# A graph network in one launch on one core: the 13 of 55 groups of source scores that GpSimd gathers are made by products of one-hots as well

## The chip, the cores and the metric

The kernel runs on one core of a Trainium2 chip. The core has five engines with queues of their own: TensorE (PE; its weight loads are listed as PEld), VectorE (DVE), ScalarE (ACT), GpSimd (POOL) and SyncE (SP, which here only issues DMAs). DMAs issued by SP and by GpSimd share 16 DMA engines. The metric is the device time of one execution in microseconds (us), lower is better.

## The reference

A graph has 3125 nodes with 512 features and 53125 edges, sorted by target (`dst`). Four residual layers follow each other, each on `h = relu(layernorm(x))`:

```python
x = x + relu(segment_sum((h @ W0)[src] * edge_weight, dst))                  # layer 0
x = x + relu(segment_sum(norm * (h @ W1.T + b1)[src], dst))                  # layer 1
x = x + relu((h + segment_sum(h[src], dst)) @ G1 + g1) @ G2 + g2             # layer 2
# layer 3, for each of 8 heads:
Wx = h @ Ws[head] + Wb[head]
s = leaky_relu(Wx[dst] @ a_w[head, :64] + Wx[src] @ a_w[head, 64:] + a_b[head], 0.2)
alpha = exp(s - segment_max(s)[dst]); alpha = alpha / segment_sum(alpha)[dst]
out = segment_sum(alpha[:, None] * Wx[src], dst)
```

What matters here is `s` of layer 3: each edge needs 8 numbers of its target node and 8 numbers of its source node. They are called target scores and source scores below.

## The kernel before, in words

The nodes are split into 25 tiles of 125. The edges are split into 440 steps (`STEPS`) of 128 edges; a step belongs to one tile of targets. A layer runs over the 440 steps: GpSimd gathers the 128 source rows of a step from a table in memory with one indirect DMA into a ring of 11 buffers (L1758 in layers 0 to 2, L1813 in layer 3), VectorE builds the step's one-hot of targets, TensorE multiplies it into the tile's sum (L1456; L1452 and L1453 in layer 2). Layer 3 also multiplies the rows by the exponentials on VectorE (L1218).

Between the steps of layer 2 and those of layer 3 lies a stage that makes the scores of all edges; it is called the score stage here, and its loop the score loop. The 440 steps form 55 groups (`NG`) of 8 steps (`UG`).

- Target scores: SP loads a group's target places, repeated over 128 partitions (`load_dst`, L1915). ScalarE makes the one-hot of them in two operations (`dst_hot`, L1337 and L1341). TensorE multiplies it with the tile's scores (L1671), one matmul a step. VectorE sums the three bf16 parts of 20 steps at once (`target_sum`, L1078). There are 22 such sums.
- Source scores, by products: a node number is split into a place (0 to 111) and a column (0 to 27, itself two digits). SP loads a group's digits, repeated over 123 partitions (`load_src`, L1923, three DMAs). VectorE makes the one-hot (`src_hot`, L1052). TensorE multiplies it with a table of 28 x 8 columns in which all columns but the right one get a very negative number (`source_product`, L1687): for a pair of steps 2 x 3 matmuls of 224 columns. VectorE takes the maximum over the 28 columns (`source_max`, L1093), once for a pair of steps, four times for a group. The banks of a pair are used again four pairs later.
- Source scores, by gathering: GpSimd gathers 8 numbers a row with one indirect DMA a step from the table of scores in memory (L1791), straight into `ue`, where the maxima go too.

Before the change the groups with `k % 4 == 3` (`GATHERED`, 13 of them, 104 steps) are gathered, the other 42 (`PRODUCTS`) are products. GpSimd issues the 104 gathers one after another when the node rows of layer 3 are done (it waits for `pj_out` and `u_st`). TensorE's, VectorE's and ScalarE's loops of this stage are written out by hand: `for k in range(NP)` runs over the product groups, and the 440 target steps are spread evenly over their pairs (`targets_till`), so that 55 target groups go with 42 source groups. The target loop of ScalarE runs over all 55 groups.

The scores of a block of 110 steps (`RS`; four blocks) are turned by TensorE with 32 matmuls (L1703, L1704) and worked on by VectorE in two halves of five operations (`edge_scores`, L1102 to L1115). `SCORES_FROM` says at which product group that begins for the first three blocks; the fourth follows the loop. TensorE waits for a block's maxima (`u_sum`), target sums (`te_sum`) and gathers (`got_u`) before it turns it.

After its score gathers GpSimd fetches 25 steps' rows of layer 3 ahead, into the space of `x` (L1805). It waits for the last load of source digits before the first of them, and for all one-hots (`dp_ok`, `sp_ok`) before the last four. The gathers of the ring (L1813) wait for the end of the fourth block (`end_rows`, VectorE L1144).

Of the kernel before, what the change touches and what calls it, by code (L numbers as in the profile page):

```python
# [26 lines left out]
def build(nc, x_in, src_in, dst_in, w_in, W0_in, W1_in, b1_in, G1_in, g1_in, G2_in, g2_in,  # L27
# [5 lines left out]
    TILES = N // TN  # L33
# [3 lines left out]
    RB = 4  # L37
    RS = STEPS // RB
# [13 lines left out]
    UG = 8  # L52
    NG = STEPS // UG
# [5 lines left out]
    PAIRS = UG // 2  # L59
# [1 line left out]
    TCS = STEPS // TC  # L61
    TH = TILES * H

    PRODUCTS = [k for k in range(NG) if k % 4 != 3]
    GATHERED = [k for k in range(NG) if k % 4 == 3]
    NP = len(PRODUCTS)
    NB = 4
    SCORES_FROM = (13, 23, 34)
    SLOPE = 0.2
    XQ = TILES // 5  # L70
    LOADED = 8
# [32 lines left out]
    with ctx:  # L104
# [3 lines left out]
        def signal(name):  # L108
            return ctx.enter_context(nc.semaphore(name))

        V, A, P, G, S = nc.vector, nc.scalar, nc.tensor, nc.gpsimd, nc.sync
# [6 lines left out]
        src_digits = nc.dram_tensor("src_digits", (3, STEPS, CE), BF16, kind="Internal").ap()  # L118
        kept_x = nc.dram_tensor("kept_x", (TILES, TN, D), F32, kind="Internal").ap()
        score_table = nc.dram_tensor("score_table", (N, H), F32, kind="Internal").ap()  # L120
# [15 lines left out]
        src_t = sb("src_t", [CE, STEPS], I32)  # L136
# [63 lines left out]
        def z16(n):  # L200
# [12 lines left out]
                          for n in range(2))  # L213
# [43 lines left out]
        ue = big[:, 4 * FW:4 * FW + STEPS * H].rearrange("p (i h) -> p i h", h=H)  # L257
# [6 lines left out]
        dp, sp, dp_hot, sp_hot = ([flat_acc[:, 2 * WR + (2 * n + q) * GW // 2:2 * WR + (2 * n + q + 1) * GW // 2].bitcast(BF16)  # L264
                                   for q in range(2)] for n in range(4))
# [66 lines left out]
        g2_tr, g2_rows, g2_z = (signal(f"g2_{n}") for n in ("tr", "rows", "z"))  # L332
# [5 lines left out]
        pj_tr, pj_hi, pj_lo, pj_z, pj_out = (signal(f"pj_{n}") for n in ("tr", "hi", "lo", "z", "out"))  # L338
# [24 lines left out]
        u_st = [signal(f"u_st{n}") for n in range(2)]  # L363
# [4 lines left out]
        far_ok = signal("far_ok")  # L368
        dp_ok, sp_ok = signal("dp_ok"), signal("sp_ok")
        te_mm, te_sum = signal("te_mm"), signal("te_sum")  # L370
        got_u = [signal(f"got_u{n}") for n in range(RB)]
        u_mm, u_sum = signal("u_mm"), signal("u_sum")
        cont_ok, cont_rep = signal("cont_ok"), signal("cont_rep")
        sc_mm, sc_z = signal("sc_mm"), signal("sc_z")
# [43 lines left out]

        def pair_step(n):

            return PRODUCTS[n // PAIRS] * UG + 2 * (n % PAIRS)

        def pairs_till(i):
            return sum(pair_step(n) < i for n in range(NP * PAIRS))

        def targets_till(n):

            return STEPS * n // (NP * PAIRS)

# [7 lines left out]
        def vector_program():  # L437
# [681 lines left out]
            beside = {}  # L1119
            for b, f in enumerate(SCORES_FROM):  # L1120
                for half in range(2):
                    scores = edge_scores(b, half)
                    for k in range(f + 3 + 2 * half, f + 5 + 2 * half):
                        beside[k] = [scores]
            for k in range(NP + 1):
                if k + 1 < NP:
                    src_hot(k + 1)
                for pair in range(PAIRS):
                    n = k * PAIRS + pair
                    if k:  # L1130
                        source_max(n - PAIRS)
                    if k < NP:
                        target_steps(targets_till(n), targets_till(n + 1))
# [268 lines left out]
        def tensor_program():  # L1402
# [115 lines left out]
            for i in range(STEPS + 14):  # L1518
# [9 lines left out]
                k = ended.get(i - 10)  # L1528
# [6 lines left out]
                k = ended.get(i - 13)  # L1535
# [94 lines left out]
            for i in range(STEPS):  # L1630
                step(2, i)
                for lag, work in ((6, turn_sums), (13, first_product), (27, turn_first), (34, second_product), (48, turn_last),
                                    (55, score_product), (Z_AT, rows_product)):
                    k = ended.get(i - lag)
# [56 lines left out]
            def edge_scores(b, half, part):  # L1691

                if half == part == 0:
                    P.wait_ge(pj_out, 3 * TILES)
                    P.wait_ge(te_sum, te_chunks(b))
                    P.wait_ge(u_sum, pairs_till((b + 1) * RS))
                    P.wait_ge(got_u[b], 16 * sum(i // RS == b for k in GATHERED for i in range(k * UG, (k + 1) * UG)))
                h0 = half * 4
                if b and part == 0:
                    P.wait_ge(sc_z, 2 * b + half - 1)  # L1700
                for j in (2 * part, 2 * part + 1):
                    to = bank[6 + half][0:RS, j * CE:(j + 1) * CE]
                    P.matmul(to, ue[:, b * RS:(b + 1) * RS, h0 + j], ident[:, :], start=True, stop=False)  # L1703
                    last = P.matmul(to, te[:, b * RS:(b + 1) * RS, h0 + j], ident[:, :], start=False, stop=True)  # L1704
                if part:
                    last.then_inc(sc_mm, 1)
# [43 lines left out]
        def gpsimd_program():  # L1750
            own = Order(g_own)

            def gather(layer):
                for i in range(STEPS):
                    n = STEPS * layer + i
                    if n >= RING:
                        G.wait_ge(stepped, step_value(n - RING))
                    G.indirect_dma_start(  # L1758
                        out=(ring16 if layer == 2 else ring)[:, n % RING, :], out_offset=None, in_=table[layer][:, :],
                        in_offset=bass.IndirectOffsetOnAxis(ap=src_t[:, i:i + 1], axis=0)).then_inc(got[n % RING], 16)  # L1760

            G.memset(ident[:, :], 0.0).then_inc(setup, 1)
            G.wait_ge(setup, 1)
            G.affine_select(out=ident[:, :], in_=ident[:, :], compare_op=ALU.not_equal, fill=1.0, base=0,
                            pattern=[[-1, 128]], channel_multiplier=1).then_inc(setup, 1)
            G.iota(iota_i[:, :], pattern=[[1, TN]], base=0, channel_multiplier=0).then_inc(setup, 1)
            G.iota(step_i[:, :], pattern=[[RS, RB]], base=0, channel_multiplier=1).then_inc(setup, 1)
            G.iota(place_i[:, :], pattern=[[0, 1]], base=0, channel_multiplier=1).then_inc(setup, 1)
            G.iota(tile_i[:, :], pattern=[[CE, TILES - 1]], base=CE, channel_multiplier=0).then_inc(setup, 1)
            G.wait_ge(step_no, 2)  # L1770
            G.wait_ge(rows_out, 16)
            for b in range(RB):
                G.indirect_dma_start(
                    out=step_rows[b].bitcast(I32), out_offset=None, in_=edge_rows[:, :],
                    in_offset=bass.IndirectOffsetOnAxis(ap=gstep[:, b:b + 1], axis=0)).then_inc(rows_in, 16)

            G.wait_ge(tables, 6)
            G.wait_ge(rows_turned, 1)
            for layer in range(3):
                for n in range(TILES * layer + TILES - 3, TILES * (layer + 1)):  # L1780
                    G.wait_ge(table_st[n % 3], table_value(n))
                gather(layer)


            for q in range(2):
                G.wait_ge(u_st[q], 16 * len(range(q, TILES, 2)))
            G.wait_ge(g2_z, TILES)
            G.wait_ge(pj_out, 3 * TILES)
            for k in GATHERED:
                for i in range(k * UG, (k + 1) * UG):  # L1790
                    G.indirect_dma_start(  # L1791
                        out=ue[:, i, :], out_offset=None, in_=score_table[:, :],
                        in_offset=bass.IndirectOffsetOnAxis(ap=src_t[:, i:i + 1], axis=0)).then_inc(got_u[i // RS], 16)


            G.wait_ge(x_kept, 32 * TILES)
            for q in range(NB):
                G.wait_ge(sp_in[q], 48 * len(range(q, NP, NB)))
            for n in range(4 * TILES - 3, 4 * TILES):
                G.wait_ge(table_st[n % 3], table_value(n))  # L1800
            for k, i in enumerate(AHEAD):
                if k == TILES - 4:
                    G.wait_ge(dp_ok, NG)
                    G.wait_ge(sp_ok, NP)
                G.indirect_dma_start(  # L1805
                    out=rows_at(i), out_offset=None, in_=table[3][:, :],
                    in_offset=bass.IndirectOffsetOnAxis(ap=src_t[:, i:i + 1], axis=0)).then_inc(got_x[AHEAD.index(i) // XQ], 16)
            G.wait_ge(end_rows, 2)
            for k, i in enumerate(ring_steps):
                n = ring_use(i)  # L1810
                if k >= RING:
                    G.wait_ge(stepped, step_value(3 * STEPS + ring_steps[k - RING]))
                G.indirect_dma_start(  # L1813
                    out=rows_at(i), out_offset=None, in_=table[3][:, :],
                    in_offset=bass.IndirectOffsetOnAxis(ap=src_t[:, i:i + 1], axis=0)).then_inc(got[n % RING], 16)

        def sync_program():
# [24 lines left out]
            for a, arr in enumerate((src_in, dst_in, w_in)):  # L1842
                e = edf if a == 2 else ed
# [72 lines left out]
                            .to_broadcast([128, GW])).then_inc(dp_in[k % NB], 16)  # L1916

            def load_src(k):
                g = PRODUCTS[k]
                if k >= NB:  # L1920
                    S.wait_ge(sp_ok, k - NB + 1)
                for a, (p0, p1) in enumerate(((0, SPL), (SPL, SA), (SA, SK))):
                    S.dma_start(sp[k % NB][p0:p1], src_digits[a, g * UG:(g + 1) * UG, :].rearrange("(a i) e -> a (i e)", a=1)  # L1923
                                .to_broadcast([p1 - p0, GW])).then_inc(sp_in[k % NB], 16)


# [94 lines left out]
```

## Time and profile before

| | us |
|---|---|
| median of 3 timed runs | 2626.45 (2623.59 to 2630.86) |
| span of the profiled execution | 3086.3 |
| of it: up to the first gather of layer 0 | 118 |
| layers 0 to 2, first to last gather | 1954 |
| score stage, last gather of layer 2 to first ring gather of layer 3 | 381 |
| layer 3 | 634 |

The profiled execution took 17.5% longer than the timed ones; no time of that execution other than its span is given. TensorE is busy in 77% of the span, GpSimd in 58%, VectorE in 52%, ScalarE in 11%. These are averages over stages that are limited in different ways: read each stage by itself, by cutting it into stretches. The busy time of GpSimd is that of issuing its DMAs. Idle time is put down either to the instruction that ended it or to "issue", when the engine waited for nothing that the profile shows.

### The profile page before, as it was taken

What the parts mean: (1) busy time and instruction counts of PE and PEld (TensorE: products, weight loads), DVE (VectorE), ACT (ScalarE), POOL (GpSimd) and SP (SyncE); (2) the same over time, 40 slices, a digit from 0 to 9 for tenths busy, and PEclk for the clock granted to TensorE, in tenths of its full rate; (3) what the DMA queues carried; (4) which work ended last, traced back from release to release, by engine and by line L of the source; (5) the groups of instructions that cost most, each with busy time, mean ns of one, the idle gap of its engine ahead of it and who ended that gap; (6) DMA issues with size and microseconds to landing.
All of it is one profiled execution on the core that took longest, in us unless ns stands there. A gap on an engine that the chain in (4) does not pass through costs nothing.

```text
span 3086.3 us, 32808 instructions
## 1 busy us (share of the span) xinstructions
PE 2384.8 (77%) x8542; PEld 1265.4 (41%) x8542; DVE 1593.7 (52%) x3774; ACT 335.0 (11%) x523; POOL 1795.9 (58%) x1878
## 2 busy tenths in 40 slices
PE   7888889887678777785788888885068589988887
PEld 5534444343223222221354454453058445544444
DVE  7665555554234353332244444444059677766665
ACT  4200000000000000000000000001057310000000
POOL 0466666665466666665666666653710456666665
PEclk9898999998789888997899999997579789999999
DMA  6586666676567766666666666663134457776665
GB/s 157 174 243 180 174 180 177 187 241 177 154 192 212 203 201 205 196 193 181 184 200 198 204 200 199 204 181 80 10 101 153 136 157 211 208 222 192 194 190 171
DMA packets 212761, 557.12 MB, mean 181 GB/s; under 512 B 55433, under 2 KB 56834, under 8 KB 212601
## 3 DMA queue, kind: packets, MB, share of 16 engines
q0 software_dynamic: 144448, 462.60, 52.3%
q1 hardware_dynamic: 66970, 90.10, 9.7%
q10 hardware_dynamic: 1182, 2.33, 0.3%
q8 instruction: 96, 1.57, 0.2%
q14 instruction: 65, 0.52, 0.1%
HBM read 515.28 MB, written 39.59 MB: 180 GB/s over the span
## 4 chain that ended last, share of the span: by engine, by line
PE 51%; DVE 15%; another core or an unknown queue 13%; issue 12%; DMA 6%; POOL 2%; ACT 1%; SPq 0%; ACTq 0%; DVEq 0%; POOLq 0%
PE tiles L1456 28%; DMA ring<-table,src_t 5%; PE upper L1416 5%; PE last_bank L1597 2%; PE tiles L1453 2%; PE tiles L1452 2%; DVE sel L776 2%; PE upper L1458 2%; PE last_bank L1416 2%; PE upper L1687 1%; POOL ring L1758 1%; PE upper L1626 1%; PE upper L1405 1%; DVE stage L713 1%
## 5 line engine op out<-in xcount | busy, mean ns | idle before, releaser
L1758 POOL DMA_INDIRECT ring<-table,src_t x1320 | 1266.9, 960 | 717.8 <-issue 324.3
L1456 PE MATMUL tiles<-ring,sel 128*125 128x512 f32 x2590 | 1390.4, 652 | 264.2 <-issue 178.4
L1456 PEld LDWEIGHTS tiles<-ring,sel 128*125 128x125 f32 x2590 | 444.3, 198 | 754.6 <-issue 745.5
L1813 POOL DMA_INDIRECT ring<-table,src_t x415 | 399.0, 961 | 240.5 <-PE upper L1458 105.5
L483 DVE TENSOR_TENSOR sel<-iota_bank,dl_t 128x500 f32<-128x500 f32 (+1 forms) x330 | 221.5, 674 | 513.3 <-PE tiles L1456 226.6
L1218 DVE TENSOR_TENSOR ring<-ring,last_bank 128x512 f32<-128x512 f32 x388 | 260.5, 685 | 169.6 <-DMA ring<-table,src_t 140.6
L1458 PEld LDWEIGHTS upper<-big,sel 128*125 128x125 f32 x880 | 169.7, 193 | 222.5 <-issue 222.0
L1452 PE MATMUL tiles<-ring,sel 128*125 128x512 f16 x440 | 176.5, 401 | 61.8 <-issue 32.1
L1453 PE MATMUL tiles<-ring,sel 128*125 128x512 f16 x440 | 172.9, 393 | 10.6 <-issue 10.3
L1416 PE MATMUL upper<-wh,hTh 128*125 128x512 f32 x200 | 100.4, 502 | 73.1 <-DVE hTl L759 23.7
L1791 POOL DMA_INDIRECT big<-score_table,src_t x104 | 98.4, 946 | 81.5 <-DVE acc L988 50.1
L776 DVE TENSOR_SCALAR sel<-node_iota,dl_t,w_t 128x125 f32<-128x125 f32 x440 | 134.2, 358 | 0.3 <-PE tiles L1456 0.2
L1458 PE MATMUL upper<-big,sel 128*125 128x8 f32 x880 | 126.2, 215 | 0.6 <-issue 0.6
L713 DVE TENSOR_TENSOR stage<-iota_bank,stage 128x500 bf16<-128x500 f32 x110 | 74.3, 676 | 86.5 <-remote 60.4
L1805 POOL DMA_INDIRECT x<-table,src_t x25 | 26.3, 1052 | 155.5 <-DMA acc<-src_digits 144.6
L1452 PEld LDWEIGHTS tiles<-ring,sel 128*125 128x125 f16 x440 | 61.2, 139 | 130.0 <-issue 111.8
L1597 PE MATMUL last_bank<-big,stage 128*125 128x512 f32 x200 | 96.8, 629 | 8.9 <-issue 7.3
L1093 DVE TENSOR_REDUCE big<-upper 128x16 f32<-128x448 f32 x84 | 50.6, 618 | 83.7 <-remote 72.4
L1405 PE MATMUL upper<-ident,stage 125*128 125x125 f32 x400 | 61.6, 277 | 41.2 <-ACT stage L1231 20.6
L1416 PE MATMUL upper<-wl,hTh 128*125 128x512 f32 x200 | 93.3, 466 | 0.0
L1416 PE MATMUL upper<-wh,hTl 128*125 128x512 f32 x200 | 92.1, 461 | 0.0
L1416 PEld LDWEIGHTS upper<-wh,hTh 128*125 128x125 f32 x200 | 45.9, 230 | 98.2 <-issue 85.0
(335 smaller groups left out, 2522.2 us busy)
## 6 DMA issues: line engine op xcount, KB each, us to landing
ring<-table,src_t POOLq DMA_INDIRECT x1735
table<-stage SPq DMA_DIRECT2D x50, 224.0 KB
table<-acc SPq DMA_DIRECT2D x50, 224.0 KB
acc<-dst_places SPq DMA_DIRECT2D x28, 256.0 KB
x<-dst_places SPq DMA_DIRECT2D x27, 256.0 KB
x<-in_x SPq DMA_DIRECT2D x25, 224.0 KB
kept_x<-x SPq DMA_DIRECT2D x25, 224.0 KB
x<-kept_x SPq DMA_DIRECT2D x25, 224.0 KB
```

Source lines behind the costliest of these rows:

```text
L483: V.tensor_tensor(to, iota_p[:, None, :].to_broadcast([CE, SB, TN]), dl_t[:, i:i + SB, None].to_broadcast([CE, SB, TN]), ALU.is_equal).the ...
L713: V.tensor_tensor(lo_hot[:, i % (2 * SB):i % (2 * SB) + SB, 0:TN], iota_p[:, None, :].to_broadcast([CE, SB, TN]), s_lo[:, i:i + SB, None]. ...
L776: V.tensor_scalar(out=sel[:, i % SELS, :], in0=node_iota[:, :], scalar1=dl_t[:, i:i + 1], scalar2=w_t[:, i:i + 1], op0=ALU.is_equal, op1=A ...
L1218: V.tensor_tensor(slot, slot, weights[:, :, None].to_broadcast([CE, H, DP]), ALU.mult).then_inc(scaled, 1)
L1416: last = P.matmul(to, a[:, q, k, :], b[:, k, :], start=(k == 0 and n == 0), stop=(k == KB - 1 and n == 2))
L1452: P.matmul(to, sel16[:, n % SELS, :], ring16[:, r, 0:D], start=False, stop=True, skip_group_check=True)
L1453: last = P.matmul(to, sel16[:, n % SELS, :], ring16[:, r, D:2 * D], start=False, stop=True, skip_group_check=True)
L1456: last = P.matmul(to, sel[:, n % SELS, :], rows, start=False, stop=True, skip_group_check=True)
L1458: last = P.matmul(upper[0:TN, bass.ds(b, 1), DEN_AT:DEN_AT + H].rearrange("p a h -> p (a h)"), sel[:, n % SELS, :], exps[:, i, :], start=F ...
L1597: last = P.matmul(bank[7][0:TN, :], yT[:, b, :], raw_w[:, b, :], start=(b == 0), stop=(b == KB - 1))
L1758: G.indirect_dma_start(out=(ring16 if layer == 2 else ring)[:, n % RING, :], out_offset=None, in_=table[layer][:, :], in_offset=bass.Indir ...
L1813: G.indirect_dma_start(out=rows_at(i), out_offset=None, in_=table[3][:, :], in_offset=bass.IndirectOffsetOnAxis(ap=src_t[:, i:i + 1], axis ...
```

## The change

All 55 groups are made by products. `NP`, the number of product groups, goes from 42 to 55; the list of gathered groups, GpSimd's 104 gathers with their waits, and TensorE's waits for them are taken out. The blocks of scores begin at groups 16, 30 and 44 of 55, where they began at 13, 23 and 34 of 42. The loops that run over `NP` now run over 55 groups, and the target steps are spread over 220 pairs, where they were spread over 168.

```diff
-    PRODUCTS = [k for k in range(NG) if k % 4 != 3]
-    GATHERED = [k for k in range(NG) if k % 4 == 3]
-    NP = len(PRODUCTS)
+    NP = NG
     NB = 4
-    SCORES_FROM = (13, 23, 34)
+    SCORES_FROM = (16, 30, 44)
...
-        got_u = [signal(f"got_u{n}") for n in range(RB)]
...
         def pair_step(n):
-            return PRODUCTS[n // PAIRS] * UG + 2 * (n % PAIRS)
+            return 2 * n
...
                     P.wait_ge(te_sum, te_chunks(b))
                     P.wait_ge(u_sum, pairs_till((b + 1) * RS))
-                    P.wait_ge(got_u[b], 16 * sum(i // RS == b for k in GATHERED for i in range(k * UG, (k + 1) * UG)))
...
-            for q in range(2):
-                G.wait_ge(u_st[q], 16 * len(range(q, TILES, 2)))
-            G.wait_ge(g2_z, TILES)
-            G.wait_ge(pj_out, 3 * TILES)
-            for k in GATHERED:
-                for i in range(k * UG, (k + 1) * UG):
-                    G.indirect_dma_start(
-                        out=ue[:, i, :], out_offset=None, in_=score_table[:, :],
-                        in_offset=bass.IndirectOffsetOnAxis(ap=src_t[:, i:i + 1], axis=0)).then_inc(got_u[i // RS], 16)
...
             def load_src(k):
-                g = PRODUCTS[k]
                 if k >= NB:
                     S.wait_ge(sp_ok, k - NB + 1)
                 for a, (p0, p1) in enumerate(((0, SPL), (SPL, SA), (SA, SK))):
-                    S.dma_start(sp[k % NB][p0:p1], src_digits[a, g * UG:(g + 1) * UG, :]...
+                    S.dma_start(sp[k % NB][p0:p1], src_digits[a, k * UG:(k + 1) * UG, :]...
```

## Rows read from the trace of the kernel before

**Rows 1.** The page: the slices of the whole span, 77 us each
```profile
PE   7888889887678777785788888885068589988887
POOL 0466666665466666665666666653710456666665
PEclk9898999998789888997899999997579789999999
```
**Rows 2.** Busy time by stretch: us, PE, PEld, DVE, ACT, POOL, clock, DMA share, GB/s
```profile
2072.00:2453.00 381.00, 210.80 (x1728) 171.30 (x1729) 188.14 (x369) 130.11 (x127) 125.91 (x131) 0.75 0.34 93
2138.00:2268.00 130.00, 13.21 (x49) 5.09 (x49) 4.14 (x7) 5.41 (x6) 86.86 (x92) 0.50 0.10 11
2268.00:2397.00 129.00, 116.47 (x1225) 109.11 (x1226) 115.54 (x208) 99.48 (x96) 0.00 (x0) 0.92 0.50 154
```
**Rows 3.** Timeline of the score stage, PE and POOL, inside the first of these stretches
```profile
2219.04 0.35 PE L1687 MATMUL tiles<-stage,acc 123*128 123x224 bf16 x1 [1.76 <-issue]
2219.26 0.94 POOL L1791 DMA_INDIRECT big<-score_table,src_t  x1 [0.30 <-issue]
2220.51 0.94 POOL L1791 DMA_INDIRECT big<-score_table,src_t  x1 [0.30 <-issue]
2221.14 0.10 PEld L1687 LDWEIGHTS tiles<-stage,acc 123*128 123x128 bf16 x1 [3.39 <-issue]
2222.54 0.34 PE L1687 MATMUL tiles<-stage,acc 123*128 123x224 bf16 x1 [3.15 <-issue]
```
**Rows 4.** Instructions by line: all gathers, duration min/median/max in ns, first and last start
```profile
L1758 POOL DMA_INDIRECT ring<-table,src_t x1320: 940/946/1642, 117.8 to 2071.9; - x189
L1791 POOL DMA_INDIRECT big<-score_table,src_t x104: 940/944/1133, 2122.9 to 2251.7; - x104
L1813 POOL DMA_INDIRECT ring<-table,src_t x415: 940/946/3199, 2452.6 to 3073.0; - x139
```
**Rows 5.** Waits of GpSimd: us in total, times, longest
```profile
POOL ring L1758 <- DMA table<-stage: 45.5, 2, 29.7
POOL ring L1758 <- DMA table<-acc: 29.7, 1, 29.7
```
**Rows 6.** Timeline of one product group on VectorE, first to next one-hot, and PE's pairs
```profile
2377.57 0.48 DVE L1052 TENSOR_SCALAR acc<-acc,digit 123x1024 bf16<-123x1024 bf16 x1
2377.97 0.62 DVE L1093 TENSOR_REDUCE big<-tiles 128x16 f32<-128x448 f32 x1
...
2378.19 0.73 PE L1687 MATMUL upper<-stage,acc 123*128 123x224 bf16 x6
...
2378.50 0.61 DVE L1093 TENSOR_REDUCE big<-iota_bank 128x16 f32<-128x448 f32 x1
...
2378.81 0.73 PE L1687 MATMUL upper<-stage,acc 123*128 123x224 bf16 x6
...
2379.56 0.65 DVE L1078 TENSOR_REDUCE ring<-tiles 128x160 f32<-128x480 f32 x1
...
2380.13 0.61 DVE L1093 TENSOR_REDUCE big<-upper 128x16 f32<-128x448 f32 x1
...
2380.66 0.48 DVE L1052 TENSOR_SCALAR acc<-x,digit 123x1024 bf16<-123x1024 bf16 x1
```
**Rows 7.** Busy time by stretch: 30 product groups, and six without scores between
```profile
2277.28:2389.41 112.13, 101.53 (x1088) 95.48 (x1087) 103.24 (x186) 88.93 (x84) 0.00 (x0) 0.94 0.52 159
2282.91:2300.71 17.80, 16.63 (x210) 15.93 (x208) 17.09 (x35) 17.54 (x17) 0.00 (x0) 1.00 0.66 206
```
**Rows 8.** Timeline: one half block of scores on VectorE, first and last of five operations
```profile
2447.45 0.68 DVE L1102 SCALAR_TENSOR_TENSOR acc<-acc 110x512 f32<-110x512 f32 x1
...
2451.27 0.69 DVE L1115 TENSOR_TENSOR acc<-acc,ring 110x512 f32<-110x512 f32 x1
```
**Rows 9.** DMA queues: 2150 to 2240 us, and 2282 to 2302 us
```profile
q0 software_dynamic: 2303, 0.30, 8.6%
...
q1 hardware_dynamic: 2274, 4.00, 63.6%
```
**Rows 10.** Timeline of VectorE: the fourth one-hot of the loop
```profile
2133.34 0.48 DVE L1052 TENSOR_SCALAR acc<-x,digit 123x1024 bf16<-123x1024 bf16 x1
```
**Rows 11.** The chain of waits, pairs of source products after a wait for VectorE
```profile
2328.16 1.21 PE iota_bank L1687 x6
2329.45 1.13 PE upper L1687 x6
2330.62 1.13 PE upper L1687 x6
```
**Rows 12.** Timeline: GpSimd's first gather ahead, its 22nd, and a one-hot beside them
```profile
2397.29 1.42 POOL L1805 DMA_INDIRECT x<-table,src_t  x1 [144.64 <-DMA acc<-src_digits]
...
2401.13 0.46 DVE L1052 TENSOR_SCALAR acc<-x,digit 123x1024 bf16<-123x1024 bf16 x1
...
2424.96 0.94 POOL L1805 DMA_INDIRECT x<-table,src_t  x1 [0.30 <-issue]
```

More of the change, by code:

```diff
@@ L1922, in load_src @@
                 for a, (p0, p1) in enumerate(((0, SPL), (SPL, SA), (SA, SK))):
-                    S.dma_start(sp[k % NB][p0:p1], src_digits[a, g * UG:(g + 1) * UG, :].rearrange("(a i) e -> a (i e)", a=1)
+                    S.dma_start(sp[k % NB][p0:p1], src_digits[a, k * UG:(k + 1) * UG, :].rearrange("(a i) e -> a (i e)", a=1)
                                 .to_broadcast([p1 - p0, GW])).then_inc(sp_in[k % NB], 16)
```

## The prediction

> **What bounds the kernel now.** I read the slices of the whole span first [rows 1]. TensorE is busy nearly everywhere except in three slices near two thirds, where it falls to 5, 0 and 6 tenths while GpSimd stands at 3, 7 and 1. That is the score stage, the only place that the change touches. Then I cut this stage into stretches [rows 2]. From the last gather of layer 2 to the first ring gather of layer 3 it takes 381 us. In it lie two opposite halves: 130 us in which TensorE starts only 49 matmuls and its clock is at 0.50 (1.2 GHz), and 129 us in which it starts 1225. The reader is to see that the first of them is exactly the time of the 104 score gathers (2122.9 to 2251.7, [rows 4]), with some 15 us of delay at either end.
>
> The timeline shows what TensorE does there [rows 3]: single weight loads and matmuls, 1.4 to 3.4 us apart, each put down to "issue", so they wait for no semaphore. VectorE and ScalarE only wait for TensorE. GpSimd issues a gather every 1.25 us (0.94 and a gap of 0.30) without a hitch. So in the profiled execution the gathers stop TensorE. Forty-nine matmuls are 49/1088 of 112.13 us [rows 7], 5 us of work, so this costs 125 us.
>
> **Is that time there in a timed run?** The whole forecast hangs on this, because the profiled execution has a span of 3086.3 us and the timed runs a median of 2626.45. The sum can be drawn up from GpSimd, which paces the layers. Its steady pitch is 1.25 us (more exactly 0.944 + 0.303 = 1.247). Layers 0 to 2 have 1320 gathers, 1646 us, and waits for tables between layers of 29.7 us, twice or so: 60 us [rows 4, 5]. Layer 3 has 415: 518 us. With 118 us before the first gather and 13 us after the last (3086.3 less 3073.0), everything but the score stage takes 2355 us at least. The timed median leaves 272 us for the score stage, where the profile shows 381. The difference is 109 us, close to the 125 of the stretch in which TensorE is stopped. If the stage took 381 us in a timed run, the total would be 2736 us. The other reading needs the gathers to be faster without a profile: at 1.185 us a gather the sum closes with a score stage of 381. No row gives such a pitch, while 1.247 is the pitch of the whole first stretch. I take the stopped time for a property of the profiled execution at 87 in 100.
>
> The Trainium skill, page "NOTIFIC — the notification-queue block", section 7.1, says that the block which writes the trace's records holds its producers back inside rather than lose a record. If that is what stops TensorE, the stop is in no timed run, which is the reading taken; no run here shows it yet.
>
> **The score loop without the stop.** Its pace is read where no gather runs. From one one-hot at 2277.28 to the 31st at 2389.41 there are 30 groups in 112.13 us, 3.74 us each [rows 7]. In it are blocks of scores: one half block takes 2447.45 to 2451.99 (the last starts at 2451.27 and lasts 0.69), 4.5 us [rows 8], so three whole blocks in the loop are 27 us. Where no scores lie between, six groups take 17.80 us, 2.97 us each. One group on VectorE [rows 6]: one-hot 0.40 (2377.57 to 2377.97) and four maxima of 0.53 (2377.97 to 2378.50), 2.53 us, and half a target sum: 0.57 (2379.56 to 2380.13) x 22/42 = 0.30. That is 2.83 of the 2.97. VectorE is busy in 17.09 of those 17.80 us, but ScalarE in 17.54: it makes 55/42 target one-hots a source group. So the pitch has 0.14 us that VectorE waits, and two engines are about even there. TensorE needs 0.63 to 0.65 a pair (2378.19 to 2378.81), 2.6 a group, and is third.
>
> **The change part by part.**
> - *Added, 13 groups on VectorE*: 13 x 2.53 = 32.9 us, all in the loop's pace. The target sums and score blocks stay as they are in number.
> - *Given back*: ScalarE now has one target group a source group, at most 17.54/17.80 x 2.97 x 42/55 = 2.2 us against 2.53 + 0.57 x 22/55 = 2.76 us on VectorE. The 0.14 us a group should go: 42 x 0.14 = 5.9 us. Sum: +27 us.
> - *Added on TensorE*: 13 x 24 matmuls, 13 x 2.6 = 34 us, beside VectorE's. TensorE then needs 4 x 0.65 = 2.6 us a group, under 2.76. This cover is thin: if it goes, the loop is TensorE's (second rival).
> - *Added on SP*: 13 x 3 loads of digits, by the same depth of four buffers. The DMA queue of SP has 63.6% of the engines where the loop runs freely [rows 9]; a source group brings 55/42 fewer target loads with it afterwards, so the rate falls. Nothing.
> - *Removed, 104 gathers of 32 bytes a row*: 130 us of GpSimd. Without the stop, is anything waiting for them? The fourth one-hot of the loop starts at 2133.34 [rows 10], the gathers at 2122.9. At 1.25 us they end at 2253, and land a few us later. The 42 groups end at 2133.34 + 38 x 2.97 + 27 = 2273. The earlier blocks ask for 24, 52 and 80 gathers, done at 2153, 2188 and 2223; the loop gets to groups 13, 23 and 34 at about 2163, 2202 and 2243. Every one is 10 to 20 us early. They take 8.6% of the DMA engines [rows 9]. Between nothing and 8.6% of the loop's 42 x 2.97 = 125 us, 0 to 10.7 us, can come back; I take 2, the end with free DMA engines being nearer.
> - *TensorE's wait for the gathers, `got_u`*: met early, as above; nothing. The moved starts of blocks keep their place relative to the steps; nothing.
> - *Gathers ahead (L1805)*: they wait for the last load of digits before and after, so they move with the end of the loop. 22 of them take 2397.29 to 2425.90, 1.30 us each [rows 12], and layer 3's ring begins 27 us later. Nothing.
>
> Sum for a timed run: 32.9 - 5.9 - 2 = +25, so 2626.45 + 25 = 2651 us. Its ends: nothing given back and the pitch of 3.74 us a group of the whole stretch, 13 x 3.74 = 48.6, so 2675; and 32.9 - 5.9 - 10.7 = 16.3, so 2643. Against the profiled execution's own time the same sum is 3086.3 - 125 + 27 = 2988 us.
>
> **The rivals.**
> - *The stop is real* (the other side). The gathers stop TensorE in timed runs too. Then the change takes away 125 us and adds 27: 2626 - 98 = 2528 us. It decides as soon as more than 27 us of the 125 are in the timed runs. For it: it stands in the trace, and TensorE alone is hit, also beside the gathers ahead. Against it: the sum above. Chance 0.13.
> - *TensorE at its lower clock becomes the bound.* After VectorE's score work TensorE comes back at pairs of 1.17 us (2329.45 to 2330.62) [rows 11], against 0.65. If such spells grow, the added groups cost 13 x 4 x 1.17 = 61 us: 2687 us. Against it: the clock is 1.00 in the free stretch. Chance 0.05.
> - *The gathers were late in timed runs.* Beside a busy VectorE 22 of them took 1.30 us each, with single ones at 1.42 [rows 12]. At 1.30 they end at 2258, still ahead of 2273; the loop is theirs from (2273 - 2123)/104 = 1.44 us on. At 1.62 us they end at 2292, 19 us late, the change costs only 25 - 19 = 6 us: 2632, no change that can be told. Chance 0.12.
>
> To this last one the page "SBUF — State Buffer" of the Trainium skill speaks, in "SBUF: two separate sides": VectorE in its two-port modes and GpSimd lock each other out of a shared pair of ports. By that rule one-hots and gathers would slow each other, which speaks for this rival. The trace hardly agrees: a one-hot beside gathers took 0.46 us, one without 0.48 [rows 6, 12].
>
> **How the numbers follow.** A measurement of this kernel can tell about 0.3%, 8 us. The forecast, 2651, has 0.70, the clock 0.05, late gathers 0.12, the real stop 0.13. Slower by over 0.3%: 0.75; within: 0.12; faster: 0.13. The range takes the forecast's own, 2643 to 2675, and goes down over the late gathers to 2618; it leaves out the stop (0.13) and the clock (0.05).
>
> **What the profile afterwards would show.** The stop from 2138 to 2268 is gone, TensorE starts some 9 matmuls a us through the loop, and the profiled span falls by about 98 us although the timed runs get longer; that pair of signs is the test of the main step. The one-hots follow each other at about 2.76 us where no scores lie between, and ScalarE has idle time there. The gathers ahead still slow TensorE at the end of the loop. The prediction is wrong if the timed runs fall with the span, or if the pitch stays at 2.97 or rises because TensorE has taken the lead.

## The result, and the profile after

The changed kernel takes 2659.06 us (2653.42 to 2662.41, 4 runs) beside 2628.05 us of the kernel before: a ratio of 1.0119, with a 95% interval of 1.0101 to 1.0137. It is slower by 31 us, where 25 us were forecast. That is the answer on the chip of this comparison. On another chip, met later, the same change makes the kernel 3% faster, and that is the larger part of what follows: the stop of TensorE in the first profile [rows 2, 3] is real on chips of that kind, and absent on this one.

The page of the changed kernel, slices of 66.5 us:

```profile
PE   6889999989688888888589999999889699998898
DVE  7686666665335454333245555555799878877776
POOL 0277777777477777777577777775000567777775
PEclk9889999999899999999789999999999799999999
```

The hole of TensorE near two thirds [rows 1] is not there, and its clock stays up. GpSimd has nothing to do in the score stage. The span is 2661.1 us, that of the times. It fell by 425 us against the first profile, though the times rose; the prediction named that pair of signs, but expected a fall of only 98 us. The experiments give the reason: there are two kinds of chip, and the first profile looks like one of the slower kind, while the times were taken on the faster. The chip of the first profile is not on record. So the pair of signs tests nothing, and the kernel before needs a second profile (the first experiment) for a comparison. Busy time by stretch of that profile (first) and of the changed kernel (second), columns as in [rows 2]: the whole score stage, from the last gather of layer 2 to the first ring gather of layer 3, and 130 us inside its loop.

```profile
1844.70:2079.00 234.30, 192.03 (x1724) 165.09 (x1723) 185.82 (x364) 130.13 (x127) 134.66 (x131) 0.93 0.55 151
1908.00:2038.00 130.00, 115.99 (x1261) 109.87 (x1260) 116.53 (x210) 102.89 (x100) 95.30 (x93) 0.96 0.62 165
```

```profile
1839.30:2103.50 264.20, 221.95 (x2037) 194.44 (x2036) 218.75 (x429) 130.13 (x127) 26.44 (x26) 0.95 0.50 145
1910.00:2040.00 130.00, 117.42 (x1266) 111.10 (x1264) 122.22 (x224) 86.76 (x84) 0.00 (x0) 0.97 0.51 150
```

The stage grows from 234.3 to 264.2 us, by 29.9, nearly all of the 31. Inside the loop TensorE starts 1261 matmuls in 130 us with 93 gathers beside it, and 1266 without them; in the first profile it started 49 in such a stretch. The other parts stay: layers 0 to 2 take 1726.9 us (117.8 to 1844.7) before and 1722.2 us (117.1 to 1839.3) after. The spans differ by less than the medians (2637.2 and 2661.1 us), because the profiled execution of the kernel before took 2638.5 us, 10 more than its median, and 5 of them lie in those layers.

A piece of the loop on VectorE, in the timeline of the changed kernel:

```profile
1907.69 0.48 DVE L1049 TENSOR_SCALAR acc<-x,digit 123x1024 bf16<-123x1024 bf16 x1
1908.08 0.62 DVE L1090 TENSOR_REDUCE big<-tiles 128x16 f32<-128x448 f32 x1
1908.61 0.65 DVE L1075 TENSOR_REDUCE ring<-tiles 128x160 f32<-128x480 f32 x1
...
1910.77 0.48 DVE L1049 TENSOR_SCALAR acc<-x,digit 123x1024 bf16<-123x1024 bf16 x1
1910.94 0.31 PE L1668 MATMUL tiles<-stage,acc 125*128 x2 [0.71 <-issue]
1911.16 0.62 DVE L1090 TENSOR_REDUCE big<-tiles 128x16 f32<-128x448 f32 x1
1911.98 0.62 DVE L1090 TENSOR_REDUCE big<-iota_bank 128x16 f32<-128x448 f32 x1 [0.19 <-PE iota_bank L1684]
...
1913.77 0.48 DVE L1049 TENSOR_SCALAR stage<-acc,digit 123x1024 bf16<-123x1024 bf16 x1
```

The first group has a target sum (L1075) and takes 3.08 us. The next has none and still takes 3.00: TensorE stood for 0.71 us at a target matmul, and VectorE had to wait for its maximum. From 1907.69 to 1945.74 there are 13 groups of 2.93 us each, where 2.76 were expected. Six of the 13 have a target sum, where 5.2 are the average; that is 0.04 us a group of the difference.

### The profile page after: what moved, and what is told of

Read it like the earlier page. It is cut to its first block, busy times and chain, and to the rows that moved or that the text cites. A ratio compares the mean times of both kernels' runs of the same rounds, so it can differ in the third digit from the quotient of the medians.

```text
span 2661.1 us, 33494 instructions
## 1 busy us (share of the span) xinstructions
PE 2304.7 (87%) x8854; PEld 1231.9 (46%) x8854; DVE 1630.1 (61%) x3839; ACT 335.2 (13%) x523; POOL 1708.5 (64%) x1774
## 4 chain that ended last, share of the span: by engine, by line
PE 54%; DMA 19%; POOL 10%; DVE 9%; issue 7%; ACT 1%; SPq 0%; ACTq 0%; DVEq 0%; POOLq 0%
PE tiles L1453 30%; DMA ring<-table,src_t 18%; POOL ring L1754 9%; PE upper L1413 5%; PE last_bank L1413 3%; PE tiles L1449 3%; PE last_bank L1594 3%; PE tiles L1450 2%; PE upper L1684 2%; POOL ring L1798 2%; PE upper L1455 1%; PE upper L1402 1%; DVE big L1090 1%; PE iota_bank L1684 1%; PE upper L1623 1%
## 5 line engine op out<-in xcount | busy, mean ns | idle before, releaser
L1453 PE MATMUL tiles<-ring,sel 128*125 128x512 f32 x2590 | 1361.6, 635 | 174.4 <-DMA ring<-table,src_t 108.7
L1453 PEld LDWEIGHTS tiles<-ring,sel 128*125 128x125 f32 x2590 | 417.6, 190 | 667.1 <-issue 659.0
L1413 PE MATMUL upper<-wh,hTh 128*125 128x512 f32 x200 | 91.2, 456 | 3.4 <-DVE hTl L467 1.8
L1594 PE MATMUL last_bank<-big,stage 128*125 128x512 f32 x200 | 90.0, 592 | 1.6 <-DVE x L715 1.6
L1265 ACT ACTIVATE acc<-tiles,dis 125x512 f32<-125x512 f32 x25 | 17.2, 687 | 552.6 <-PE tiles L1453 552.6
L1267 ACT ACTIVATE acc<-tiles 125x512 f32<-125x512 f32 x25 | 14.9, 598 | 541.5 <-PE tiles L1450 541.5
L1263 ACT ACTIVATE acc<-tiles 125x512 f32<-125x512 f32 x25 | 14.9, 598 | 536.4 <-PE tiles L1453 536.4
L1413 PE MATMUL upper<-wl,hTh 128*125 128x512 f32 x200 | 81.4, 407 | 0.0
L1413 PE MATMUL upper<-wh,hTl 128*125 128x512 f32 x200 | 81.2, 406 | 0.0
```

The costliest lines, as they stand in the source:

```text
L1413: last = P.matmul(to, a[:, q, k, :], b[:, k, :], start=(k == 0 and n == 0), stop=(k == KB - 1 and n == 2))
L1453: last = P.matmul(to, sel[:, n % SELS, :], rows, start=False, stop=True, skip_group_check=True)
L1594: last = P.matmul(bank[7][0:TN, :], yT[:, b, :], raw_w[:, b, :], start=(b == 0), stop=(b == KB - 1))
```

## The experiments

The line numbers of a variant differ by a few from those of the kernel it starts from. The runs fell on four chips, each met once. On one of them the kernel before takes 2631 us (2624 to 2635 in 23 runs); on three it takes 3118, 3089 and 3120 us (3084 to 3128 in 38 runs). The first is called the faster kind below, the others the slower kind; whether that is a property of the chip or of a state that it was in, the runs can't tell. A ratio is always to the kernel before on the same chip.

**A second profile of the kernel before.** Nothing is edited.

> The kernel before, unchanged, to have a second profile of it beside its times. My theory (the stop of TensorE beside the score gathers belongs to the one profiled execution of 3086 us, not to the kernel): a span near 2627 us, TensorE runs through the 104 gathers at some 9 matmuls a us, one-hots 2.97 us apart where no scores lie between, the score loop ends at least 10 us after the last gather has landed. Rival (the stop is real, as the chance of 0.13 had it): the 130 us with some 49 matmuls are there again, whatever the span.

2628.86 us, 0.9994 (0.9985 to 1.0004). Instructions by line, and the waits of TensorE from 1900 to 2065 us:

```profile
L1791 POOL DMA_INDIRECT big<-score_table,src_t x104: 939/947/2349, 1893.9 to 2030.4; - x104
L1093 DVE TENSOR_REDUCE big<-upper x84: 592/612/626, 1902.8 to 2064.3; 128x16 f32<-128x448 f32 x84
L1805 POOL DMA_INDIRECT x<-table,src_t x25: 945/949/1782, 2039.2 to 2073.2; - x25
```

```profile
PE tiles L1671 <- issue: 11.8, 17, 2.0
PE tiles L1687 <- DVE big L1093: 10.3, 4, 6.6
PE upper L1687 <- DVE big L1093: 1.3, 2, 0.7
```

There is no stop and no wait for a gather. The last gather starts at 2030.4, the last maximum at 2064.3: the gathers are 34 us early by their starts, some 30 if one takes 3.8 us to land as a gather of the ring does, and not 20. Two sizes were off and nearly cancelled: a gather costs 1.33 us beside a busy VectorE (136.5 us for 103 intervals), not 1.25, and the loop from the fourth one-hot (1903.8) to the end takes 161 us, not 140.

**The gathers alone, in both kernels.** First, the kernel before without them:

```diff
                 for i in range(k * UG, (k + 1) * UG, 4):
-                    G.indirect_dma_start(out=ue[:, i, :], ...)
+                    G.memset(ue[:, i:i + 4, :], 0.0).then_inc(got_u[i // RS], 1)
```

> The kernel before with its 104 score gathers replaced by 26 fills with zeros on GpSimd: 42 groups of products, 13 groups of source scores that are not computed. It prices the gathers alone. My theory (hidden work that takes a small share of the DMA engines): 2628 - 2 us, anything from 2617 to 2629. Rival (the gathers were late for the scores, or held TensorE or VectorE up): the loop gets shorter by more than 11 us, 2617 us or less.

2630.7 us, 1.0001 (0.9992 to 1.0010): the gathers cost nothing that the times can tell; the interval still holds the 2 us that the sum gave back for them. The profiled score stage is 233.1 us (1836.2 to 2069.3) beside 234.3. Then the changed kernel with them:

```diff
+            for n, i in enumerate(i for k in range(3, NG, 4) for i in range(k * UG, (k + 1) * UG)):
+                if n >= 8:
+                    G.wait_ge(got_junk[n % 8], 16 * (n // 8))
+                G.indirect_dma_start(out=junk[:, n % 8, :], ...)
```

> The changed kernel, all 55 groups by products, with the 104 gathers put back: same place on GpSimd, same table and rows, but into a small tile that nobody reads, each waiting for the one eight before. It adds the gathers where nobody waits for them. My theory: 2659 + 2 us, at most 2670. Rival (beside a loop that VectorE and TensorE fill, gathers cost by ports or DMA engines, so that the change gave back more than 2 us): 2670 us or more.

2662.37 us, 1.0117 (1.0102 to 1.0131) beside 1.0119 of the changed kernel: again nothing that can be told. Its score stage is 266.4 us (1839.9 to 2106.3) beside 264.2. On this chip the change is 13 groups of products in exchange for something that costs some 1 to 2 us by the traces.

**More gathers: 18 groups.**

```diff
-    PRODUCTS = [k for k in range(NG) if k % 4 != 3]
+    PRODUCTS = [k for k in range(NG) if k % 3 != 2]
-    SCORES_FROM = (13, 23, 34)
+    SCORES_FROM = (12, 21, 30)
```

> The other way round: 18 of 55 groups gathered (every third) and 37 by products; the scores of the blocks begin at groups 12, 21 and 30. 40 gathers more than before, 50 us at 1.25 us each, and 5 product groups fewer. My theory (the gathers were about 20 us early before, so they become the bound): the last block waits for them, 50 - 20 = 30 us later, 2658 us. Rival (gathers are hidden at this number too, only products cost): 5 x 2.97 = 15 us less, 2613 us.

2647.3 us, 1.0068 (1.0055 to 1.0081): 18 us slower, not 30. The waits of TensorE, 1880 to 2110 us, and GpSimd's waits in the ring of layer 3, in the second profile of the kernel before and in this run:

```profile
PE upper L1703 <- DMA big<-score_table,src_t: 33.9, 3, 22.1
```

```profile
POOL ring L1813 <- PE upper L1458: 63.5, 149, 18.3
```

```profile
POOL ring L1813 <- PE upper L1458: 46.0, 148, 1.0
```

Here the gathers are the bound: TensorE stands 22.1 us at the last block of scores until they have landed. GpSimd goes on to its gathers ahead and to the ring without a pause between, and layer 3 begins 39 us later than before (a stage of 273.4 us, 1835.1 to 2108.5). But 21 of them come back in layer 3, 536.9 us instead of 558.2: the one wait of 18.3 us that GpSimd had there, once the ring was full, is gone. The sum of 30 us left this slack out: 40 gathers at 1.31 us are 52 us, and in the kernel before GpSimd waits 7.8 us before its gathers ahead, 4.9 after them and 18.3 in the ring. That leaves 21, near the 18 measured.

**Who paces the loop of 55 groups.** The maxima of the changed kernel over half the columns, and two of the three parts of each product. Both fell on a chip of the slower kind (3118 us), so the first was run again beside the changed kernel on another of that kind (3089 us):

```diff
-  bank[2 + n % 4][:, 0:2 * CTH].rearrange("p (i t h) -> p i h t", i=2, h=H),
+  bank[2 + n % 4][:, 0:2 * CTH].rearrange("p (i t h) -> p i h t", i=2, h=H)[:, :, :, 0:CT // 2],
```

```diff
-                    for part in range(3):
+                    for part in range(2):
```

> The changed kernel with the maxima of the source scores (L1090) taken over 14 of the 28 columns: the same 220 operations of VectorE over half the numbers, so part of the maximum is left out. It asks who paces the loop with 55 groups. Price on VectorE: 224 of 448 numbers, some 0.23 us of each 0.53, 220 times, 51 us. My theory (VectorE paces, TensorE is right behind with 2.52 us a group and its stalls at the loading of tile numbers, about 2.75 in all against 2.93 measured): only 10 to 20 us come back, 2640 to 2650 us. Rival (VectorE alone paces): some 50 us, 2610 us.

> The changed kernel with two of the three bf16 parts of each source product (L1684): 16 instead of 24 matmuls a group, the lowest part of the scores is left out. A pair then takes TensorE about 0.44 instead of 0.63 us. My theory (VectorE paces): only the stalls go, at most 55 x 0.2 = 10 us, 2649 to 2657 us. Rival (TensorE has taken the lead, the thin cover of the prediction): 220 x 0.19 = 42 us, 2617 us.

> The changed kernel with maxima over 14 of 28 columns, as in e4_half_max (part of the maximum is left out), now beside the changed kernel itself on the same chip. My theory as there (VectorE paces, TensorE is right behind): 10 to 20 us under the changed kernel. Rival (VectorE alone paces): 50 us under it.

Half the maxima: 0.9636 (0.9606 to 0.9666) and, again, 0.9637 (0.9611 to 0.9664), beside 0.9692 (0.9669 to 0.9716) of the changed kernel on that chip; 2978.04 beside 2994.57 us, 16.5 us less. Two parts: 0.9677 (0.9643 to 0.9711), which would be 5 us less; the intervals, taken on different chips, don't tell that from nothing nor from 20 us. The traces are closer: the score stage is 284.5 us in the changed kernel, 272.3 and 270.8 with half the maxima, and 287.9 with two parts. So taking away a third of TensorE's source matmuls gives nothing, far from the 42 us of the rival, and taking away 51 us of VectorE (0.39 instead of 0.62 us, 220 times) gives 16.5. VectorE paces and TensorE is right behind, as expected. Stretches inside the loop, of two parts and of half the maxima (again):

```profile
2172.00:2302.00 130.00, 101.86 (x1008) 91.97 (x1005) 125.06 (x233) 90.43 (x87) 0.00 (x0) 0.91 0.52 157
```

```profile
2170.00:2290.00 120.00, 114.13 (x1219) 109.83 (x1215) 91.74 (x216) 80.04 (x76) 1.78 (x2) 1.00 0.50 151
```

In the first VectorE is busy in 125.1 of 130 us, in the second TensorE in 114.1 of 120: each is full when the other is relieved.

**Less work for ScalarE**, on the kernel before:

```diff
-                own.mark(A.activation(dp[k % NB][0:TN], dp[k % NB][0:TN], ACT.Abs, bias=less_place[0:TN, :]))
-                A.wait_ge(a_own, own.n)
```

> The kernel before without the first of the two ScalarE operations of a target one-hot (L1337): ScalarE has about 1.1 us less for each of 55 groups, and the target one-hots come out wrong. It tests the term of the prediction that ScalarE held the loop of 42 groups up by 0.14 us a group. As predicted: 42 x 0.14 = 6 us less, 2623 us. Rival (ScalarE was only nearly as busy and held nobody up, and the 5.9 us were never there to be given back): 2629 us, no change.

3113.84 us beside 3118.35, 0.9986 (0.9969 to 1.0002). It fell on a chip of the slower kind, and its interval holds both the 6 us and none. Its trace settles the term all the same: 130 us from 15 us after the first score gather on, then the same 30 groups and the same six as in [rows 7].

```profile
2162.00:2292.00 130.00, 13.38 (x50) 5.17 (x50) 4.14 (x7) 3.31 (x4) 86.98 (x92) 0.51 0.08 10
2301.80:2413.99 112.19, 101.62 (x1088) 95.53 (x1087) 103.24 (x187) 46.85 (x44) 0.00 (x0) 0.94 0.51 159
2307.43:2325.23 17.80, 16.64 (x210) 15.94 (x208) 17.09 (x35) 9.23 (x9) 0.00 (x0) 1.00 0.69 212
```

The six groups take 17.80 us with ScalarE busy for 9.23 of them, and took 17.80 with ScalarE busy for 17.54; the 30 groups take 112.19 and took 112.13. ScalarE held nobody up. The first line shows another thing: this kernel is the kernel before but for one operation of ScalarE, it takes 3108 to 3123 us in its 12 runs, and its TensorE starts 50 matmuls in 130 us beside the gathers, as the first profile has 49. Its score stage takes 384.7 us (2093.0 to 2477.7), there it was 381. That is why the first profile is taken for one of a chip of the slower kind.

**15 groups gathered.**

```diff
-    PRODUCTS = [k for k in range(NG) if k % 4 != 3]
+    PRODUCTS = [k for k in range(NG) if k % 11 not in (3, 6, 10)]
-    SCORES_FROM = (13, 23, 34)
+    SCORES_FROM = (13, 23, 33)
```

> 15 of 55 groups gathered (three of each eleven), 40 by products; scores of the blocks begin at groups 13, 23 and 33. Two product groups fewer than before, 16 gathers more. In the second profile of the kernel before, GpSimd has some 33 us to spare on its way to the first rows of layer 3 that are used: 9 us before its gathers ahead, 6 after them, 18 when the ring is full; 16 gathers at 1.32 us take 21 of it. My theory (GpSimd's slack covers them, products cost 2.5 us a group): 5 us less than before, 2624 us. Rival (the last block of scores or the gathers ahead come late at once): 2630 us or more.

3133.61 us, 1.0045 (1.0025 to 1.0064), on the same chip as the last. What it would do on the faster kind stays open. On this one it is 14 us slower, and a sum fits that: 16 gathers more prolong the stop by 16 x 1.25 = 20 us, two product groups fewer give back 5.

**The changed kernel beside the kernel before on a chip of the slower kind.** Nothing is edited.

> The changed kernel, unchanged, beside the kernel before on whatever chip comes. The last four kernels met a chip on which the kernel before takes 3118 us in all its runs and TensorE is stopped beside the 104 score gathers, as in the first profile. My theory (the stop belongs to some chips, there it is in every run): on such a chip the change takes off about 125 us and adds 30, some 3025 us, 0.97 of the kernel before; on a chip of the other kind 2659 us, 1.012. Rival (the change costs 30 us everywhere, and the stop is made up elsewhere): 1.01 on either kind.

2994.57 us beside 3088.57: 0.9692 (0.9669 to 0.9716), 94 us faster. The score stage and 130 us inside its loop:

```profile
2068.30:2352.80 284.50, 226.56 (x2037) 196.65 (x2036) 219.78 (x431) 130.14 (x127) 26.00 (x26) 0.91 0.46 135
2150.00:2280.00 130.00, 118.45 (x1272) 112.54 (x1269) 122.13 (x224) 83.98 (x79) 0.00 (x0) 0.97 0.51 151
```

The stage takes 284.5 us, against 381 in the first profile [rows 2], which has the span and the stop of this kind of chip: 96 us less. Without gathers the loop runs on this chip as it does on the other, 1272 matmuls in 130 us beside 1266. The 20 us that the stage is longer than there come at its end, where the 25 gathers ahead run: the last one-hot follows the one before it after 21.6 us (2306.0 to 2327.7), on the faster kind after 3.2.

**The gathers put back on such a chip, and the gathers spaced.** First the changed kernel with 104 gathers that nobody waits for, the same edit as above; then the kernel before with a pause after each gather:

```diff
                         in_offset=bass.IndirectOffsetOnAxis(ap=src_t[:, i:i + 1], axis=0)).then_inc(got_u[i // RS], 16)
+                    G.memset(pause[:, :], 0.0).then_inc(paused, 1)
+                    pauses += 1
+                    G.wait_ge(paused, pauses)
```

> The changed kernel with the 104 score gathers put back into a tile that nobody reads, as in e2_55_and_gathers, in the hope of a chip of the slower kind (kernel before near 3090 to 3120 us). Nothing waits for these gathers there, so what they cost is neither a wait nor lateness. My theory (the gathers themselves stop TensorE on such a chip): about 115 to 125 us over the changed kernel's 0.969 of the kernel before, so 1.006 to 1.010 of it, some 3110 to 3120 us. Rival (it is the wait for the gathers that holds TensorE): 0.97. On a chip of the faster kind 1.012 again.

> The kernel before with a fill of a small tile (128 x 128) after each of the 104 score gathers, which GpSimd waits for: gathers some 1.7 instead of 1.25 us apart, so that they end some 45 us later. On a chip of the slower kind: if TensorE is stopped because gathers follow each other without a gap, it runs part of the time now and the kernel gains up to 50 us on the kernel before, 0.985 or less. Rival (each gather costs TensorE its time, whatever lies between): the stop is as large or lasts longer, 1.00 or more. On a chip of the faster kind the gathers eat up the slack and the kernel is 5 to 15 us longer than before.

3141.17 us, 1.0077 (1.0048 to 1.0105), and 3089.15 us, 0.9906 (0.9875 to 0.9937), beside 3119.82 us. The stretch of the gathers in the one and in the other:

```profile
2140.00:2270.00 130.00, 16.18 (x112) 11.38 (x112) 10.06 (x20) 9.27 (x10) 96.28 (x102) 0.54 0.19 35
```

```profile
2155.00:2295.00 140.00, 66.81 (x434) 46.56 (x433) 37.65 (x66) 39.74 (x41) 112.80 (x192) 0.56 0.25 61
```

In the first nothing waits for the gathers, and TensorE is stopped all the same: 112 matmuls in 130 us, 69 of them in the first 16 us, before it sets in. The gathers raise the ratio from 0.9692 to 1.0077, some 120 us. It is the gathers that stop TensorE, not a wait. In the second the gathers are 1.46 us apart (2143.2 to 2293.8 for 103 intervals) instead of 1.25 (1.7 were expected), and TensorE starts 3.1 matmuls a us instead of 0.4, unevenly: up to 75 in 8 us, and then again 16 to 20. It is still far from the 9.8 of a loop without gathers. The kernel gains 31 us by having GpSimd do more. The other reading, that each gather costs TensorE its time whatever lies between, falls; but three quarters of the stop are still there, and no run says how large a gap ends it.

## Why the prediction was right, and where not

*Sign and size on the chip of the comparison* were right: 31 us against 25, inside 2643 to 2675 and not far off its middle.

*Thirteen groups at 2.53 us* was the step that carried it, and it held: from the fourth one-hot to the last there are 38 groups in 148.8 us before (1903.8 to 2052.6) and 51 in 181.1 us after (1898.4 to 2079.5), 32.3 us for 13 groups, 2.48 each. (Against the kernel without gathers, 147.6 us, it is 33.5 and 2.58.) After the last one-hot the loop needs 2 us less than before, which makes 29.9.

*Given back by ScalarE, 5.9 us*, was the term that was mis-sized: it is nothing. ScalarE was busy in 17.54 of 17.80 us there [rows 7], and that was taken for holding VectorE up. With half of ScalarE's work taken away the same groups take the same 17.80 us, and in the changed kernel it is busy in 86.8 of 130 us and the groups still take 2.93. VectorE's one wait in those 17.80 us is 0.50 us for a product of TensorE, and TensorE's pauses before target matmuls are there in both kernels (6.7 us in those 30 groups before, 8.3 us in 51 groups after). What ends such a pause the profile doesn't show. By the prediction's own sign, a pitch that stays at 2.97, this step failed: 2.93 is hardly less. Without it the sum would have been 31 us.

*The gathers are hidden and cost at most 10.7 us*: hidden, and worth 1 to 2 us, by two runs in the two kernels. The rival of late gathers is out too, on the faster kind: they would have to be some 30 us longer. The prediction priced it at 1.30 us a gather, from 22 gathers in [rows 12]; up to 2424.96 those are 21, at 1.38 us. Measured were 1.33.

*TensorE as the bound*: not so, but the cover of 2.6 us under 2.76 was as thin as the prediction said. TensorE's pauses reach VectorE, so neither engine is wholly hidden. That the gathers ahead slow TensorE at the end of the loop holds on the slower kind only.

*The stop is no part of the timed runs*, on which the whole forecast hung. The arithmetic was right for the runs it was made against: 2626 us leave no room for it. The reading of it was wrong. It is not a property of being profiled: on either kind of chip the profiled execution is about as long as the others (2638.5 us beside a median of 2628.9, and 3118.8 beside 3113.8). By all that the runs show, the sum compared a profile of one kind of chip with times of another. The rival that "the stop is real", priced at minus 98 us, is what happens on the slower kind: minus 94 us. The sign of the forecast rests on the result having been timed on the same kind of chip as the 2626 us; three of the four chips that the experiments met were of the other, so that is luck in part. By the page "NOTIFIC — the notification-queue block" of the Trainium skill, section 7.1, the writing of records could hold an engine back; what was seen speaks for no such cause, since the profile without the stop has as many records (32808 instructions in either profile of the kernel before) and unprofiled executions on the slower kind are as long as profiled ones.

*The 2355 us for all but the score stage* were a lower bound by GpSimd's pitch and came out at 2403 (2637.2 less 234.3). The 272 us left for the stage were 234. The closeness to the 125 us of the stop was in part luck.

## What to carry to other kernels

Where a profile's span and the times disagree by more than a few per cent, the profile may be of a chip that behaves otherwise: profile again before anything is argued from its idle time, and compare ratios only within one chip. Work that an idle engine does beside the bound, like these gathers, is worth what the bound engine saves, 2.5 us a group here on the faster kind of chip, until its own end comes late (at 18 groups it did). An engine that is busy in 17.5 of 17.8 us need not hold anybody up: ScalarE here did not. And where two engines are even, relieving one of them gives a third of its time, 16.5 of 51 us here.

## What the runs showed of the hardware that I had not expected

- Two kinds of chip, or of states of a chip. The kernel before takes 2631 us on one and 3089 to 3120 us on three; without a score gather in the loop both run it at 9.8 matmuls a us. Layers 0 to 2, where GpSimd gathers all the time, take 1722 us on the one and 1951 us (117.6 to 2068.3) on the other with the same changed kernel, and layer 3 takes 558 and 633. So the stop beside the score gathers is only part of the difference: the changed kernel, which has none of them, is still 325 us longer by its spans, 20 of them in the score stage.
- On the slower kind TensorE, and only TensorE, falls to 49 or 50 matmuls in 130 us, with gaps of 1.4 to 3.4 us between its instructions and single ones of 15.3 us, some 15 us after the score gathers begin to follow each other at 1.25 us (2122.9 to 2138, 2146.9 to 2162), and recovers as long after them. At 1.46 us apart a quarter of the lost time is gone. VectorE's and ScalarE's operations keep their length beside it. What in the chip makes the difference stays open; no run here tells the instruction supply of TensorE from any other path that it shares with the gathers.
- Beside a busy VectorE the gathers are longer on the faster kind (1.02 us on average, 2.35 at most, against 0.95 in the stopped stretch), as the page "SBUF — State Buffer" of the Trainium skill, section "SBUF: two separate sides", lets expect. Of the 16 gathers out of 104 that took over 1.00 us, 11 are among the 21 that overlap the operations of a block of scores (L1102 to L1115); the longest overlaps the scan of L1111. The price for the kernel is some 1 to 2 us.
